# Three small reorderings in block 1: single-row waits before VectorE's marks, the second norm's root and spread at earlier beats, the last table load ahead of the squares

## The reference, cut to what matters

```python
dots = einsum('bhid,bhjd->bhij', l2norm(q), l2norm(k)) * QK_SCALE   # 16 heads, 4 memory keys
dots = einsum('hg,bgij->bhij', W_pre_th, dots)                      # heads mixed
dots = where(causal, mask_value, dots)
vk = top_k(dots, 64)[0][..., -1:]                                   # the 64th largest of each row
dots = where(dots < vk, mask_value, dots)                           # the rest is dropped
attn = einsum('hg,bgij->bhij', W_post_th, softmax(dots))            # heads mixed back
...
x = _layernorm(x + attention(x)); x = _layernorm(x + ffn(x))
```

## Time and profile before

| | |
|---|---|
| median of three runs | 3628.78 us (3628.4, 3628.78, 3636.17) |
| profiled execution, its own time | 3634.36 us |
| its span | 3633.1 us |
| mean granted TensorE clock | 0.98 |
| block 1's ranking of the first sequence begins | 846.7 us |
| busy: PE, DVE, ACT, POOL | 3390.1, 3437.1, 3092.9, 1745.4 us |

### The profile page before, as it was taken

One profiled execution on the slowest core, in us unless ns is written; L12 is line 12 of the kernel. 1 busy time (PEld: TensorE's weight loads), 2 busy tenths in 40 slices (PEclk: granted clock), 3 DMA queues, 4 the chain that ended last, 5 costly groups with the idle time before them and its releaser, 6 DMA issues.

```text
span 3633.1 us, 78764 instructions
## 1 busy us (share of the span) xinstructions
PE 3390.1 (93%) x19287; PEld 2527.5 (70%) x19287; DVE 3437.1 (95%) x18664; ACT 3092.9 (85%) x10837; POOL 1745.4 (48%) x3670
## 2 busy tenths in 40 slices
PE   4999999986999999999999999999999999999987
PEld 2888888863666666676676666666666666666665
DVE  7999999936999999999999999999999999999993
ACT  6888888856898899989899898998998998898863
POOL 0000000014666666666666666666666666666663
PEclk9999999997999999999999999999999999999998
DMA  3000000002222222222222222222222222222210
GB/s 132 11 14 13 13 12 13 10 13 85 73 71 78 82 66 65 65 66 66 66 65 66 74 71 70 74 73 79 79 66 65 65 66 65 67 65 66 73 55 4
DMA packets 254141, 210.74 MB, mean 58 GB/s; under 512 B 78000, under 2 KB 234736, under 8 KB 252912
## 3 DMA queue, kind: packets, MB, share of 16 engines
q1 hardware_dynamic: 253680, 205.70, 18.1%
HBM read 93.97 MB, written 111.67 MB: 57 GB/s over the span
## 4 chain that ended last, share of the span: by engine, by line
PE 66%; ACT 17%; DVE 11%; issue 4%; POOL 2%; DMA 0%; SPq 0%; DVEq 0%; ACTq 0%; POOLq 0%
PE bank L378 10%; PE bank L221 8%; PE bank L1434 6%; PE bank L1422 5%; PE bank L1407 5%; PE bank L1465 3%; PE bank L469 3%; PE bank L195 3%; ACT SN L1618 3%; PE bank L1499 3%; DVE W L1826 3%; PE bank L1479 3%; PE bank L1438 3%; PE bank L346 3%; ACT sq L496 2%
## 5 line engine op out<-in xcount | busy, mean ns | idle before, releaser
L1826 DVE MATCH_REPLACE8 W<-last,W 128x130 f32<-128x130 f32 (+18 forms) x3456 | 871.9, 259 | 0.0
L1848 DVE MAX8 last<-W 128x8 f32<-128x130 f32 (+18 forms) x3456 | 762.9, 262 | 0.0
L1933 POOL TENSOR_SCALAR posts<-post,share 128x128 f32<-128x128 f32 x1024 | 366.7, 378 | 284.0 <-DVE share L1755 279.1
L1602 ACT ACTIVATE T<-T,peak 128x260 f32<-128x260 f32 (+15 forms) x1024 | 410.9, 409 | 3.5 <-POOL T L1984 2.4
L1618 ACT ACTIVATE SN<-bank,rq 128x260 f32<-128x260 f32 (+1 forms) x1024 | 357.9, 424 | 61.3 <-PE bank L1407 60.8
L1422 PE MATMUL bank<-T,pre 128*128 128x40 f32 (+15 forms) x1024 | 365.3, 439 | 14.4 <-ACT T L1626 10.1
L1434 PE MATMUL bank<-posts,T 128*128 128x128 f32 (+7 forms) x2048 | 311.7, 289 | 68.9 <-POOL posts L1933 60.6
L1984 POOL TENSOR_TENSOR T<-T,below 128x520 f32<-128x520 f32 (+12 forms) x416 | 360.3, 882 | 20.0 <-DVE below L1857 4.6
L1434 PEld LDWEIGHTS bank<-posts,T 128*128 128x128 f32 (+7 forms) x2048 | 249.0, 174 | 165.3 <-POOL posts L1933 88.9
L938 DVE TENSOR_TENSOR_SCAN hs<-dA,dx 128x256 f32<-128x256 f32 x512 | 349.9, 684 | 2.9 <-ACT dA L800 1.9
L1949 POOL TENSOR_TENSOR T<-T,w_mask 128x32 f32<-128x32 f32 x512 | 141.1, 278 | 412.6 <-ACT T L1626 410.2
(11 more groups left out here) (242 smaller groups left out, 9572.3 us busy)
## 6 DMA issues: line engine op xcount, KB each, us to landing
scores_by_token<-SN SPq DMA_DIRECT2D x64, 520.0 KB, 2.6
scores_by_token<-SN SPq DMA_DIRECT2D x64, 396.0 KB, 3.1
scores_by_token<-SN SPq DMA_DIRECT2D x32, 780.0 KB, 3.3
scores_by_token<-SN SPq DMA_DIRECT2D x32, 264.0 KB, 2.6
scores_by_token<-SN SPq DMA_DIRECT2D x32, 260.0 KB, 2.0
T<-scores_by_token SPq DMA_DIRECT2D x32, 244.0 KB, 3.0
T<-scores_by_token SPq DMA_DIRECT2D x32, 228.0 KB, 3.2
T<-scores_by_token SPq DMA_DIRECT2D x32, 212.0 KB, 3.8
```

Of the source, the lines that this page charges most:

```text
L1602: act.activation(one, one, ACT.Exp, bias=peak[k % 2][:, j:j + 1], accum_out=total[k % 4][:, j:j + 1]).then_inc(e_made, 1)
L1826: dve.match_replace(both[:, s, at:to], best[n], both[:, s, at:to], LOWEST).then_inc(ranked, 1)
L1848: dve.max(best[n], both[:, s, at:to]).then_inc(ranked, 1)
L1933: pool.tensor_scalar(posts[(4 * k + j) % NP][:], post[:], share[k % 2][:, j:j + 1], 1.0, ALU.mult, ALU.mult).then_inc(posts_made, 1)
```

## The change

Four places. Each of VectorE's two marks of a quad waits for the threshold of its own row, where the first mark waited for both. The refinement of the second root stands at beat 116 of GpSimd's table instead of 118, its spread at beat 111 of TensorE's instead of 114. For the last sequence only, ScalarE loads the table for Ln and Exp before it copies and squares, not after.

```diff
-    PE_SPREAD2 = 114
+    PE_SPREAD2 = 111
...
-    POOL_ROOT2 = 118
+    POOL_ROOT2 = 116
...
                 if (b := whose(p, t, ACT_SQUARE2, 2)) is not None:
+                    if b == SEQS - 1:
+                        table(EXP_LN)
                     nd.act_square(act, b)
...
             if j0 in CUT[i]:
                 out = mark_of(g, j0)
-                dve.wait_ge(found_wide, 2 * ((QUADS + 1) * b + i + j0 // 2 + 1))
                 if drops(k, DROPS[i][0]) > 1:
                     dve.wait_ge(dropped, drops(k, DROPS[i][0]) - 1)
                 for n, (j, s) in enumerate(rows):
+                    dve.wait_ge(found_wide, 2 * ((QUADS + 1) * b + i + j0 // 2) + n + 1)
                     dve.tensor_scalar(out[:, s, :], x[:, s, :], best[n][:, 7:8], DROP, ALU.is_lt, ALU.mult).then_inc(cut_marked, 1)
                     yield
```

## The result

| kernel | median | runs | profiled execution (span) |
|---|---|---|---|
| before | 3628.31 us (3619.96 to 3636.17) | 20 | 3634.36 (3633.1) |
| changed | 3634.34 us (3631.73 to 3639.38) | 20 | 3634.27 (3632.9) |

The ratio is 1.0018, 95% interval 1.0012 to 1.0024: the change costs about 6.5 us, a real loss whose middle lies just under the bound of 0.2% (the interval reaches over it). The forecast was 3629 and "within 0.2%".

What follows compares the result with a forecast made beforehand. Two loops of nearly equal length, TensorE with ScalarE and VectorE with GpSimd, bound the period. 30 x (0.07 - 0.02) = +1.5, first and last sequence -0.88, table load -0.58: 0.0 us, so 3629, range 3618 to 3637.

Steps and rivals of the forecast that it cites:

- its own signs: Trace signs: hold under 0.1 us before TensorE's L134, undisturbed periods 84.7 to 84.9 us, wrong below 84.6 or above 85.0.
- third rival: On TensorE the weight load must run out before the spread: hold 0.35 us a period, +8.4 us, 3637.2; chance 0.13.
- Two loops: TensorE with ScalarE, and VectorE with GpSimd's last drop, meet at quad 7's first exponential; the second is longer by 0.02 us.
- loop A: The chain of TensorE with ScalarE through one period of block 1, put at 84.73 us.
- first rival: VectorE's gain from the marks arrives whole in the period: 14.7 us less, 3614; chance 0.12.
- The spread's hold: TensorE waits for GpSimd's root before the moved spread: 0.07 us a period, bounds 0 and 0.35.
- What was called hidden: Later premix copy on ScalarE (some 0.1 us), GpSimd's mask (up to 0.4 us) and key projection cost the period nothing.
- Six waits for `x_d`: VectorE's six waits for the spread, 6.6 us in all, vanish without the total falling.
- second rival: An earlier spread spares VectorE 6.6 + 2.0 us of waits; with the table load 9.2 us less, 3619.6; chance 0.05.
- The table load: At the program's end ScalarE's load of 1.30 us fits into 1.65 us of idling, so L122 begins 0.58 us earlier.
- The sum: Periods +1.5, first and last sequence -0.88, table load -0.58 us: together 0.0 us.

Runs made afterwards that it cites:

- late spread: Changed kernel with the spread back at beat 114, behind the key projection: 3622.86 us, 0.9980 of before.
- spacer: Changed kernel plus one useless VectorE max over 355 columns ahead of quad 7's ranking: 3626.02 us, 0.9998 of before.
- root and spread: Kernel before with only the root at beat 116 and the spread at beat 111: 3631.71 us, 1.0005 of before.
- spread alone: Kernel before with the spread at beat 111 and the root left at 118: 3653.69 us, 1.0066 of before.
- behind premix: Changed kernel with the spread one step later on TensorE, between the 232-column premix and the key projection: 3618.48 us, 0.9968 of before; repeated, 0.9982.

## Why the prediction was right or wrong

*The forecast as a whole.* By the time it holds: 1.0018 is within 0.2%, 3634.34 within 3618 to 3637. By its own signs it does not: it wanted a hold under 0.1 us before L134 and measured is 0.24, and it called itself wrong above 85.0 us a period and measured is 85.03. A quarter of a microsecond was missed in every undisturbed period, nearly the third rival's sum, and that the time still stayed under the bound of 7.3 us is luck.

*Two loops, and the marks.* Right. With the marks alone the period falls to loop A's length and no further, with a wait at the reciprocal of 0.36 us in each. The 0.44 us each in the first and the last sequence can't be told from the scatter (the last period went from 87.8 to 86.9 in this pair, but is 88.9 in late spread, which has the marks too). The mark starts 0.09 us early as forecast. Loop A is 84.69 us and not 84.73, so 0.07 us of the gain arrives in a period and not 0.02. The first rival (VectorE's gain whole, 3614) is out: periods did not go to 84.3, except with TensorE lightened. The passage of the Trainium skill, "VectorE: DVE Perf Modes", section "The DRAIN you can't avoid", by which the prediction had the marks save nothing, did not hold at this place: 0.12 us a pair were saved (0.03 after to 0.09 before). The same section adds that a next instruction that is not held starts earlier, and that half is what the rows show; the prediction left it out.

*The spread's hold.* This is the term that was mis-sized: 0.07 forecast, 0.34 measured, where 30 x 0.27 us are 8 us. The step that failed is "In the new order they follow the drop, which ends at 1942.04 + 1.51 = 1943.55, so the root is ready at 1944.59". It took GpSimd's drop, marks and all, at its old length from a trace in which VectorE was not yet ahead, although the same change puts it ahead; and it priced the hold up to the spread's start alone, with nothing for a spread whose weights come late. Behind a drop of today's length the hold would have been about what was said: the spacer restores that length and has none. Four kernels lie on one line, period = 84.69 + 0.10 + hold: spacer 0 (84.79), root and spread 0.09 (84.88), changed 0.24 (85.03), spread alone 0.95 (85.75); and "behind premix", where weights can be loaded ahead, 84.69 without the 0.10. (The spacer ran on the other chip, where "behind premix" has 84.73: there the line gives 84.83, 0.04 above the measured.) So every part of 0.34 has its experiment: 0.10 weight load, 0.09 GpSimd's marks at 1.54 in the new order (why they are not at 1.44 was not tested), 0.15 by VectorE being ahead.

*The third rival* had the right sum and half the mechanism. It said 0.35 us and 3637.2, because "the weight load must run out first". The load costs 0.10, not 0.28; the rest is the late root. I had kept the bound and taken 0.07 because in the earlier trace rows the spread starts 0.05 us after the root. It does here too (1942.26 + 0.19, then 1942.51: 0.06). What rows 11 could not show is the step behind the start, 0.55 instead of 0.44, since nothing stands behind the spread there.

*What was called hidden.* It was: hold and weight load make up the whole 0.34 us, and the line above leaves nothing that can be seen for the premix copy, the mask and the key projection. VectorE's wait for the mask did grow, from 10.6 to 18.3 us, but that is TensorE's lateness handed on by GpSimd: spread alone, with GpSimd's order untouched, has 18.4.

*Six waits for `x_d`.* As forecast: 6.6 became 1.4 us and VectorE's waits in all did not fall. The second rival is out: root and spread, which has none of them, is no faster than before.

*The table load.* Right in size: 0.62 for 0.58, read from the rows, since the time can't show it. The Trainium skill, "ScalarE: Activation LUTs", section "What ACT_TABLE_LOAD costs", has 1.38 us follow the load; here the next instruction starts 0.36 us after it, when TensorE's result is there, and not later.

*The sum.* Forecast 0.0, with 30 x 0.05 of it from the periods. With the terms of the traced pair: 30 x 0.27 - 0.9 - 0.6 = +6.7 us, and the medians differ by 6.0, the ratio by 6.5. Two of these terms are softer than they look: the 0.9 is one pair's last period, and a disturbed period is 86.3 us long in both kernels, so it loses next to nothing. With 25 undisturbed periods and without the 0.9 it is 6.8 - 0.6 = 6.2 us. The profiled pair, equal to 0.1 us, would have confirmed the forecast of 0.0, wrongly: its +6.7 were hidden by 5.0 us less of disturbed periods and 1.4 us less before the first reciprocal.

## What to carry to other kernels

When a change lets one engine run ahead, every duration that you take from the old trace for another engine is open, if the two meet in time somewhere: look which instructions will newly lie beside each other. A consumer moved directly behind its producer pays the hold and also the preparation that used to overlap (here 0.10 us of weight load); put one short independent instruction between them. And compare medians of undisturbed periods before spans: two spans agreed here to 0.1 us while the kernels differed by six.

## What the hardware showed that I had not expected

**VectorE's `TENSOR_TENSOR` and GpSimd get in each other's way.** GpSimd's mark grew from 0.68 to 0.92 us when VectorE's pairing was running at its start, and VectorE's pairing from 0.39 to 1.25 us when GpSimd's add had begun 0.11 us before it; it then ended 0.2 us after the add. A `MAX8` in the same place did nothing. The Trainium skill states a cause: "SBUF — State Buffer", sections "SBUF: two separate sides" and "Who interferes with whom", has the two engines share one pair of ports that whichever starts first holds exclusively for its whole instruction; a VectorE instruction with two SBUF inputs contends for it with a GpSimd one that reads SBUF, while one with at most one such input, outside the two-port modes, does not. No run here shows a port. The rows agree in who waits in these two places and in the exemption of `MAX8`, which has one input. They differ twice: a full block until 1938.65 and then 0.68 us would end at 1939.33, but GpSimd's mark ended at 1939.11; and a pairing of VectorE's that begins 0.4 us into a mark of GpSimd's (before, and in the spacer) takes its usual 0.30 us, though the mark has 0.30 us yet to run.

**Where the clock falls.** The granted clock of TensorE falls to the lower of its two levels (1.2 of 2.4 GHz) for some microseconds. Within the 30 periods it does so in nearly every case at the same place: within 0.3 us of the start of L1407, before which TensorE is idle for 0.65 us. Root and spread, TensorE's timeline and two windows that meet there:

```profile
1944.39 1.02 PE L1407 MATMUL bank<-kT,qT 64*128 64x260 f32 x4 [0.65 <-ACT SN L1618]
1945.34 1.03 PE L1422 MATMUL bank<-T,pre 128*128 128x200 f32 x2
1946.17 1.91 PE L1434 MATMUL bank<-posts,T 128*128 128x128 f32 x8
```

```profile
1945.04:1948.44 3.40, 3.40 (x17) 3.10 (x16) 3.40 (x32) 1.56 (x6) 1.78 (x7) 0.56 0.58 235
1941.00:1944.40 3.40, 2.64 (x18) 1.43 (x16) 3.37 (x18) 3.11 (x12) 2.16 (x5) 1.00 0.39 157
```

From 1.00 to a mean of 0.56 (the window reaches 0.4 us past the dip, which itself is at 0.50), and L1434's eight passes in 1.91 us where they take 1.04 otherwise. Nearly each such dip makes one disturbed period, and in nearly every case with the whole work done that period is 86.3 us long, whatever the undisturbed one is: 84.69 + 1.62, 84.88 + 1.43, 85.03 + 1.29, 85.75 + 0.56. Behind the dip TensorE is late anyway and no longer held at the spread (in spread alone the 0.80 us of idle before L134 is missing in such periods), so a hold costs nothing there. Every period has that idle time, and only 2 to 9 of 30 have the dip; why just these stays open.
